# Two-layer gated cross-attention network on one core: in layer 0, two steps of TensorE put the per-token work last, and the sums of experts 4 to 7 are taken in other steps

## The chip, the cores and the metric

One Trainium2 chip (trn2), one core, one launch. The metric is the device time in microseconds; of the kernel before, three runs were taken, and their median is 2502.51 us (2501.88 to 2504.15). TensorE is called PE here, VectorE DVE, ScalarE ACT, GpSimd POOL and SyncE SP, as in the profile.

## What is computed

The input is 16 sequences (batches) of 256 tokens with 256 features, and a context of the same shape. Two layers follow each other; each is a cross-attention to the context and then a feed-forward part, both added to the stream through a tanh gate. The change lies wholly in layer 0:

```
x = x + tanh(g) * attention0(layernorm(x), ctx)      # 16 heads of 64, causal and padding mask
# layer 0, feed-forward, per token:
h = rmsnorm(layernorm(x));  q = h @ Wq + bq;  kv = (h @ Wdown + bdown) @ Wup + bup
att = softmax_over_g(q[head h] . k[head g] / 4)       # 16 x 16 scores of one token's own heads
x' = n + (sum_g att * v[head g]) @ Wo + bo            # n is layernorm(x)
h2 = rmsnorm(x');  gate = softmax(h2 @ Wg + bg)       # 8 experts
x = x + tanh(g) * (x' + sum_e gate_e * (h2 @ We[e]))
```

Layer 1 has an attention with 16 heads of 16 and a feed-forward part of three hidden products of 1024; the change doesn't touch it. Of layer 0's products, those marked hi and lo in the trace are three products each (a number is split in two parts, `product3`, lines 155 to 163).

## The kernel before, in words

**A software pipeline over batches.** In each round of layer 0 every engine works on three batches at once, a stage for each: the cross-attention of batch a, the per-token attention ("mix") of batch b = a-1, and the experts ("moe") of batch c = a-2; some projections of batch a+1 are made ahead. A round is the `body` of each engine (POOL from line 387, ACT, DVE, and PE from line 1021). It goes through 20 steps, s = 0 to 19 (STEPS = H + LAG_V = 20), roughly one attention head a step, with a beginning (BEGIN, BEGIN_OUT) and an end. Rounds 0, 1 and 2 are written out, rounds 3 to 14 are a hardware loop, and rounds 15 to 17 are written out again. The written-out ones from 15 on are merged with layer 1's programs by the numbers that the programs yield (`side_by_side`); SP's program yields 17 before the store of batch 13.

**Order on an engine.** Every engine executes its instructions in the order in which `body` writes them, so a wait holds up all that stands behind it. The engines meet by semaphores. What has to be followed:

- PE in a step: the scores of two heads in even steps (`pair_scores`, lines 945 to 948), then `beside_head` (the work of batches b and c), then the transposes of one head's probabilities (`head_transpose`, lines 955 to 957; in step 3 those of head 0 stand before `beside_head`), in odd steps from 5 on the value products of two heads (`pair_values`, lines 968 to 971), and then a projection: k3, v1, v3, q2, q3 of batch a in steps 0, 1, 2, 3, 5, and k0, xT, k1, v0, k2, v2 of batch a+1 in steps 9, 10, 11, 13, 16, 19. After step 19 comes the output projection (`attn_out`, line 980), and then the next round begins with the transposes of `o` (line 879, "oT"), q0, q1 and the product with `fo` ("out").
- `beside_head` on PE: step 2 transposes h; step 3 makes the per-token queries ("q", x is hT and w is fq); step 4 the down projection ("down") and the transposes of y ("h2T"); step 5 half of the up projection ("up0") and the gate's logits ("gate", wg); step 6 the other half ("up1"). An expert's product (`we0` to `we7`, 12 matmuls) is made in the steps of `expert_at`.
- DVE in a step: the masked scores and their maximum (`attn_max`, line 745), the reciprocal of the sum of the head before (`attn_sum`, line 751), and `beside_head`: adding bq to the queries (639), the low half of dT (645), adding bup to kv (651), an expert's gated sum into `acc` in the steps of `add_at` (`moe_experts`, line 729), the reduction of POOL's products to the per-token scores (`mix_scores`, line 655, in steps 7, 9, 11 and 12), its softmax (maximum 662 and subtraction 664 in step 12; sum 668, reciprocal 670 and multiplication 672 in step 13), and `mix_gather` (line 678) in steps 15, 16, 18 and 19.
- ACT in a step: transposed probabilities out of PSUM (485), exponential (468, 470), normalisation of the head before (476, 477), and, at the end of the step, the copies of projections (460), the exponential and scale of the gate (515 and 520 in steps 5 and 6), and the exponential of the per-token softmax (524, step 12).
- POOL: four multiplications of queries and keys (line 371), each of half a tile of tokens' heads, and four of weights and values (line 385, `weigh`), the first of which waits for the softmax (line 672); between the rounds the mask (354 to 358), powers (337) and the split of the context (344, 346).
- SP: the store of a batch (line 293) waits for `x2_ready`, which DVE gives after the sum of expert 7; behind it in SP's queue stand the loads of x, context and mask of a later batch (275, 278, 282).

**PSUM banks.** Products go to banks in rotation, and a user of a bank waits until the one before has been copied out. `attn` has two banks: the order of its uses is q0, q1, k3, v1, v3, T0, q2, T1, T2, q3, T3, ... (T0 is the transposes of head 0), after six uses that are made ahead. So k3, v3, q2 and T2 are in one bank, and v1, T0, T1 and q3 in the other. `side` has two banks too, in the order oT, out, hT, q, down, h2T, up0, gate, up1, we0 to we7, idle. `score` has three, `heads` one.

Of the kernel before, what the change touches and what calls it, by code (L numbers as in the profile page):

```python
# [121 lines left out]
def first(batch):  # L122

    return isinstance(batch, int) and batch == 0


def wait_apart(engine, passed, sem, value):

    engine.wait_ge(sem, value)
    engine.sem_inc(passed, 1)  # L130
# [36 lines left out]
def layer0(nc, ins, x2, left, right, both):  # L167
# [51 lines left out]
    attn = Banks(nc, left, both, "l0_attn", attn_uses + ["out"], ahead=["xT", "k0", "k1", "k2", "v0", "v2"])  # L219

    mix_at = {2: "hT", 3: "q", 4: "down", 5: "up0", 6: "up1"}
    expert_at = {6: 0, 7: 1, 8: 2, 10: 3, 12: 4, 14: 5, 15: 6, 17: 7}
    add_at = {7: 0, 8: 1, 9: 2, 10: 3, 12: 4, 14: 5, 15: 6, 17: 7}
    score_at = {7: 0, 9: 1, 11: 2, 12: 3}

    gather_at = {15: 0, 16: 1, 18: 2, 19: 3}
# [44 lines left out]
    def sync(sp):  # L271
        def load(b):
            if not first(b):
                sp.wait_ge(xn_ready, b)
            sp.dma_start(xin[:], ins["x"][bass.ds(b, 1)][0]).then_inc(x_in, 16)
            if not first(b):
                sp.wait_ge(ctx_ready, b)
            sp.dma_start(ctxin[:], ins["ctx"][bass.ds(b, 1)][0]).then_inc(ctx_in, 16)

            if not first(b):  # L280
                wait_apart(sp, sp_passed, mask_ready, b)
            sp.dma_start(maskbits[:], ins["mask"][bass.ds(b, 1)].to_broadcast([P, S])).then_inc(mask_in, 16)

        def load_residual(b):

            if not first(b):
                sp.wait_ge(x1_copied, b)
                sp.wait_ge(h_ready, b)
            sp.dma_start(x1[:], ins["x"][bass.ds(b, 1)][0]).then_inc(xres_in, 16)

        def store(b):
            sp.wait_ge(x2_ready, b + 1)
            sp.dma_start(x2[bass.ds(b, 1)][0], acc[:]).then_inc(x2_stored, 16)

        load(0)
        for k, (src, _hi, _lo, rows) in enumerate(splits):
            if k >= 2:
                sp.wait_ge(split_lo, k - 1)
            sp.dma_start(stage[0:rows, k % 2, 0:src.shape[1]], src).then_inc(raw_in[k % 2], 16)
            if k == 1:  # L300
                for dst, src in params:
                    sp.dma_start(dst, src).then_inc(params_in, 16)
            if k == 2:
                load_residual(0)
                sp.dma_start(wo[:].rearrange("p c n -> p (c n)"), ins["wo"]).then_inc(wo_in, 16)
            if k == 3:
                load(1)
        load(2)
        load_residual(1)
        with sp.Fori(3, B) as b:  # L310
            load(b)
            load_residual(b - 1)
            store(b - 3)
        load_residual(B - 1)
        yield 17
        store(B - 3)
        yield 40.6
        store(B - 2)
        yield 52
        store(B - 1)  # L320
# [549 lines left out]
    def tensor(pe):  # L870
        T = nc.tensor

        def transpose4(banks, use, batch, src):

            ps, full, free, turn = banks.at(use, batch)
            pe.wait_ge(free, turn)
            for c in range(ND):
                for t in range(NT):
                    last = T.transpose(ps[:, c * S + t * P:c * S + (t + 1) * P], src[:, t, c * P:(c + 1) * P], ident[:])
            last.then_inc(full, 1)  # L880

        def features(use, a, w, x):

            j = int(use[1:])
            ps, full, free, turn = attn.at(use, a)
            pe.wait_ge(free, turn)
            for u in range(2):
                m = slice((2 * j + u) * P, (2 * j + u + 1) * P)
                last = product3(nc, ps[:, u * S:(u + 1) * S],
                                [(w[0][:, c, m], w[1][:, c, m], x[0][:, c, :], x[1][:, c, :]) for c in range(ND)])  # L890
            last.then_inc(full, 1)

        def values(j, a):
            t, m = j // 2, slice((j % 2) * 512, (j % 2 + 1) * 512)
            ps, full, free, turn = attn.at(f"v{j}", a)
            pe.wait_ge(free, turn)
            product3(nc, ps[:], [(cT[0][:, c, t * P:(t + 1) * P], cT[1][:, c, t * P:(t + 1) * P], wv[0][:, c, m], wv[1][:, c, m])
                                 for c in range(ND)]).then_inc(full, 1)
# [24 lines left out]
        def moe_experts(c, j):  # L923
            moe_product(f"we{j}", c, [w[:, :, j * D:(j + 1) * D] for w in we], D)
# [58 lines left out]
        def project(use, a):  # L983

            if use == "xT":
                pe.wait_ge(xn_ready, a + 1)
                transpose4(attn, "xT", a, xn)
            elif use[0] == "q":
                features(use, a, wq, xT)
            elif use[0] == "k":  # L990
                if use == "k0":
                    pe.wait_ge(ctx_ready, a + 1)
                features(use, a, wk, cT)
            else:
                values(int(use[1:]), a)

        def beside_head(b, c, s):

            if b is not None and s in mix_at:
                use = mix_at[s]  # L1000
                if use == "hT":
                    pe.wait_ge(h_ready, b + 1)
                    transpose4(side, "hT", b, h)
                elif use == "q":
                    side.emptied(pe, "hT", b)
                    tokens(side, "q", b, hT, fq, D)
                elif use == "down":
                    mix_down(b)
                else:
                    mix_up(b, int(use[2:]))  # L1010
            if c is not None:
                if s == 4:
                    pe.wait_ge(h2_ready, c + 1)
                    transpose4(side, "h2T", c, y)
                elif s == 5:
                    side.emptied(pe, "h2T", c)
                    moe_product("gate", c, wg, E)
                elif s in expert_at:
                    moe_experts(c, expert_at[s])

        def body(a, b, c, nxt):
            yield BEGIN
            if c is not None:
                pe.wait_ge(gathered, 4 * (c + 1))
                transpose4(side, "oT", c, o)
            if a is not None:
                attn.emptied(pe, "xT", a)
                project("q0", a)
                project("q1", a)
            yield BEGIN_OUT  # L1030
            if c is not None:
                side.emptied(pe, "oT", c)
                tokens(side, "out", c, foT, fo, D)
            if a is not None:
                attn.emptied(pe, "v2", a)
                attn.emptied(pe, "q0", a)
            for s in range(STEPS):
                yield s
                if a is not None and s < H and s % 2 == 0:
                    if s % 4 == 0 and s > 0:  # L1040
                        attn.emptied(pe, f"q{s // 4}", a)
                    if s == 12:
                        attn.emptied(pe, "k3", a)
                    pair_scores(a, s)
                if a is not None and s == LAG_T:
                    head_transpose(a, 0)
                beside_head(b, c, s)
                if a is not None:
                    if LAG_T < s < H + LAG_T:
                        head_transpose(a, s - LAG_T)  # L1050
                    if s >= LAG_V0 and s % 2 == 1:
                        if s - LAG_V0 == 8:
                            for use in ("v1", "v3"):
                                _, _, emptied, turn = attn.at(use, a)
                                wait_apart(pe, pe_passed, emptied, turn + 1)
                        pair_values(a, s - LAG_V0)
                    if s in own_at:
                        project(own_at[s], a)
                if nxt is not None and s in ahead_at:
                    project(ahead_at[s], nxt)  # L1060
            yield STEPS
            if b is not None:
                side.skip(pe, "idle", b)
            if a is not None:
                score.skip(pe, "idle0", a)
                score.skip(pe, "idle1", a)
            if a is not None:
                heads.emptied(pe, "o2", a)
                heads.emptied(pe, "o3", a)
                attn_out(a)  # L1070
# [835 lines left out]
```

## Time and profile before

| | |
|---|---|
| median of three runs | 2502.51 us |
| the profiled execution's own time | 2502.84 us |
| its span in the trace | 2501.0 us |
| mean granted clock of PE | 0.961 |
| busy: PE, DVE, ACT, POOL | 89%, 59%, 51%, 41% of the span |

The first half of the span is layer 0, about 78 us a round; rounds of layer 1 follow from some 1300 us on. The profile gives a start and a duration to each instruction, the idle time of its engine before it in brackets, and behind "<-" the instruction that ended this idle time. A matmul of the same length lasts about twice as long when the granted clock is 0.5. Ends of matmuls are modelled and overlap with the next start, so for PE the distance from start to start is the better measure.

### The profile page before, as it was taken

The numbers are of one execution on the slowest core, as the hardware profiler recorded it, in microseconds if no ns is written. First come the engines' busy times: TensorE is split into PE (matmuls) and PEld (weight loads), VectorE is DVE, ScalarE is ACT, GpSimd is POOL, SyncE is SP. The second block draws the span as 40 slices with busy tenths as digits, with TensorE's granted clock in tenths as the row PEclk, the third lists the DMA queues.
The fourth block names the chain that finished last, engine by engine and source line by source line (L and its number), as shares of the span: only waits on it lengthen the run. The fifth ranks groups of instructions, "written<-read, shape, count | busy, mean of one in ns | idle before, by whom it ended". The sixth has DMA issues, their size and how long they took to land.

```text
span 2501.0 us, 47888 instructions
## 1 busy us (share of the span) xinstructions
PE 2227.4 (89%) x16000; PEld 1887.5 (75%) x16000; DVE 1480.4 (59%) x3922; ACT 1267.7 (51%) x3969; POOL 1023.1 (41%) x907
## 2 busy tenths in 40 slices
PE   5888899898888888888875799999999999999998
PEld 4667677777777777777664688888888888888888
DVE  4466666767667676676767635555555555555551
ACT  5655655556555565555633434455544444445541
POOL 1255555565555655556446213333332322333320
PEclk9999999999999999999977799999999999999999
DMA  4000000000000000000110200000000000000000
GB/s 154 8 12 14 6 17 17 17 13 4 17 17 17 13 4 17 17 17 4 39 32 13 110 16 7 13 17 17 17 17 17 17 17 16 5 13 17 17 9 9
DMA packets 26000, 51.40 MB, mean 21 GB/s; under 512 B 6160, under 2 KB 7312, under 8 KB 24784
## 3 DMA queue, kind: packets, MB, share of 16 engines
q1 hardware_dynamic: 25936, 50.57, 6.0%
q8 instruction: 37, 0.61, 0.1%
q14 instruction: 27, 0.22, 0.0%
HBM read 42.17 MB, written 8.39 MB: 20 GB/s over the span
## 4 chain that ended last, share of the span: by engine, by line
PE 57%; DVE 15%; ACT 8%; POOL 6%; issue 6%; DVEq 4%; POOLq 2%; DMA 0%; ACTq 0%
PE l_ffn L1714 13%; POOL l_prod L385 5%; PE l_ffn L161 4%; PE l_attn L161 4%; PE l_ffn L162 4%; PE l_ffn L163 4%; PE l_attn L1675 4%; PE l_attn L163 3%; PE l_attn L162 3%; DVEq L735 3%; PE l_side L161 3%; PE l_heads L1689 2%; POOLq L355 2%; PE l_side L163 2%; PE l_side L162 2%
## 5 line engine op out<-in xcount | busy, mean ns | idle before, releaser
L1253 POOL TENSOR_SCALAR l_probs<-l_probs,l_rinv 128x256 f32<-128x256 f32 x512 | 240.3, 484 | 479.2 <-DVE l_rinv L1492 478.3
L1376 ACT ACTIVATE l_probs<-l_score,l_negmax 128x256 f32<-128x256 f32 x512 | 239.1, 474 | 268.2 <-DVE l_negmax L1487 268.1
L385 POOL TENSOR_TENSOR l_prod<-l_att,l_kv 128x2048 f32<-128x2048 f32 x64 | 288.5, 4542 | 164.6 <-DVE l_att L672 164.6
L371 POOL TENSOR_TENSOR l_prod<-l_q,l_kv 128x2048 f32<-128x2048 f32 x64 | 291.2, 4561 | 150.7 <-DVE l_att L655 86.6
L1714 PE MATMUL l_ffn<-l_w,l_hid 128*128 128x256 f32 x1536 | 348.6, 381 | 1.0 <-ACT l_hid L1337 1.0
L1714 PEld LDWEIGHTS l_ffn<-l_w,l_hid 128*128 128x128 f32 x1536 | 286.2, 190 | 48.8 <-issue 12.7
L1499 DVE COPY l_probsT<-l_attn 128x512 f32<-128x512 f32 x240 | 164.5, 686 | 142.8 <-PE l_attn L1675 142.8
L745 DVE CUSTOM_DVE_ANT_0 l_probs<-l_score,l_mbias 128x256 f32<-128x256 f32 (+1 forms) x512 | 161.3, 352 | 144.9 <-PE l_score L947 95.8
L678 DVE TENSOR_REDUCE l_h<-l_prod 128x128 f32<-128x2048 f32 x64 | 146.3, 2286 | 107.5 <-POOL l_prod L385 107.2
L468 ACT ACTIVATE l_probs<-l_probs,l_negmax 128x256 f32<-128x256 f32 x256 | 130.8, 511 | 107.7 <-DVE l_negmax L745 106.6
L1487 DVE TENSOR_REDUCE l_negmax<-l_score 128x2 f32<-128x512 f32 x256 | 175.0, 684 | 15.0 <-PE l_score L1663 13.7
L485 ACT COPY l_probsT<-l_attn 128x384 f32<-128x384 f32 x256 | 120.9, 472 | 112.8 <-PE l_attn L957 112.7
L1337 ACT ACTIVATE l_hid<-l_ffn,l_b 128x256 f32<-128x256 f32 x384 | 162.1, 482 | 19.4 <-PE l_ffn L163 18.1
L1675 PE MATMUL l_attn<-l_ident,l_probs 128*128 128x128 f32 x1024 | 157.1, 279 | 11.4 <-DVE l_probsT L1499 6.6
L161 PE MATMUL l_side<-l_we_hi,l_h2T_hi 128*128 128x256 f32 x512 | 159.8, 312 | 2.2 <-DVE l_acc L729 1.8
L161 PE MATMUL l_attn<-l_cT_hi,l_wk_hi 128*128 128x256 f32 x384 | 124.0, 323 | 40.6 <-DVE l_xT_lo L609 39.0
L655 DVE TENSOR_REDUCE l_att<-l_prod 128x128 f32<-128x2048 f32 x64 | 145.8, 2279 | 5.0 <-issue 4.4
L162 PE MATMUL l_side<-l_we_lo,l_h2T_hi 128*128 128x256 f32 x512 | 147.5, 288 | 0.0
L163 PE MATMUL l_side<-l_we_hi,l_h2T_lo 128*128 128x256 f32 x512 | 147.1, 287 | 0.0
L476 ACT ACTIVATE l_probs<-l_probs,l_rinv 128x256 f32<-128x256 f32 x256 | 127.6, 498 | 24.3 <-DVE l_rinv L751 24.3
L1675 PEld LDWEIGHTS l_attn<-l_ident,l_probs 128*128 128x128 f32 x1024 | 118.8, 143 | 25.4 <-issue 12.4
L1238 POOL TENSOR_TENSOR l_rstdF<-l_varF,l_neghalf 128x2 f32<-128x2 f32 x16 | 11.2, 701 | 303.1 <-DVE l_varF L1421 303.1
(261 smaller groups left out, 7177.2 us busy)
## 6 DMA issues: line engine op xcount, KB each, us to landing
l_ctxin<-in_ctx SPq DMA_DIRECT2D x32, 256.0 KB, 3.0
l_xin<-in_x SPq DMA_DIRECT2D x16, 256.0 KB, 2.6
l_x<-in_x SPq DMA_DIRECT2D x16, 256.0 KB, 2.6
x<-l_acc SPq DMA_DIRECT2D x16, 256.0 KB, 2.0
l_xin<-x SPq DMA_DIRECT2D x16, 256.0 KB, 3.1
l_x<-x SPq DMA_DIRECT2D x16, 256.0 KB, 2.6
out<-l_x SPq DMA_DIRECT2D x16, 256.0 KB, 2.0
l_hid<-in_w SPq DMA_DIRECT2D x2, 1536.0 KB, 8.2
```

What stands on the lines that cost most here:

```text
L161: last = nc.tensor.matmul(out, wh, xh, start=n == 0, stop=False)
L162: last = nc.tensor.matmul(out, wh, xl, start=False, stop=False)
L163: last = nc.tensor.matmul(out, wl, xh, start=False, stop=n == len(terms) - 1)
L371: nc.gpsimd.tensor_tensor(prod[:, u].rearrange("p (h g d) -> p h g d", h=half, g=H), q4[:, u * half:(u + 1) * half].unsqueeze(2).to_broadc ...
L385: nc.gpsimd.tensor_tensor(prod[:, u].rearrange("p (h d g) -> p h d g", h=half, d=HD), a4.unsqueeze(2).to_broadcast([P, half, HD, H]), v4.u ...
L1253: last = nc.gpsimd.tensor_scalar(probs[:, j % 4, t * S:(t + 1) * S], probs[:, j % 4, t * S:(t + 1) * S], rinv[:, j, t:t + 1], 1.0, ALU.mul ...
L1337: last = nc.scalar.activation(hid[:, c, :], ps[:, u * S:(u + 1) * S], ACT.Relu, bias=b1[:, c:c + 1])
L1376: last = nc.scalar.activation(probs[:, s % 4, t * S:(t + 1) * S], ps[:, t * S:(t + 1) * S], ACT.Exp, bias=negmax[:, s, t:t + 1], accum_out ...
L1487: V.tensor_reduce(negmax[:, j], ps[:].rearrange("p (t k) -> p t k", t=NT), axis=AX.X, op=ALU.max, negate=True).then_inc(max_ready, 1)
L1499: V.tensor_copy(probsT[:, j % RING, :], ps[:]).then_inc(free, 1)
L1675: last = T.transpose(ps[:, kt * S + t * P:kt * S + (t + 1) * P], probs[:, j % 4, t * S + kt * P:t * S + (kt + 1) * P], ident[:])
L1714: last = T.matmul(ps[:, 0:D], hid[:, c, t * P:(t + 1) * P], w2[:, c, :], start=c == 0, stop=c == 3 * NHC - 1)
```

## The change

The per-token queries in step 3, and up0 and the gate's logits in step 5, are issued by PE last in their step: behind q2's projection, and behind T2, the value products of heads 0 and 1 and q3's projection. Expert 4 is made in step 13 for step 12, and expert 6 in step 16 for step 15; experts 5 and 7 keep their steps. DVE adds experts 4 to 7 in steps 14, 15, 17 and 18 for 12, 14, 15 and 17, so that steps 12 and 13 have no sum of an expert. SP's program yields 18.5 for 17 ahead of the store of batch 13.

```diff
-    expert_at = {6: 0, 7: 1, 8: 2, 10: 3, 12: 4, 14: 5, 15: 6, 17: 7}
-    add_at = {7: 0, 8: 1, 9: 2, 10: 3, 12: 4, 14: 5, 15: 6, 17: 7}
+    expert_at = {6: 0, 7: 1, 8: 2, 10: 3, 13: 4, 14: 5, 16: 6, 17: 7}
+    add_at = {7: 0, 8: 1, 9: 2, 10: 3, 14: 4, 15: 5, 17: 6, 18: 7}
...
         load_residual(B - 1)
-        yield 17
+        yield 18.5
         store(B - 3)
...
                     head_transpose(a, 0)
-                beside_head(b, c, s)
+                if s not in (3, 5):
+                    beside_head(b, c, s)
                 if a is not None:
                     if LAG_T < s < H + LAG_T:
                         head_transpose(a, s - LAG_T)
...
                     if s in own_at:
                         project(own_at[s], a)
+                if s in (3, 5):
+                    beside_head(b, c, s)
                 if nxt is not None and s in ahead_at:
                     project(ahead_at[s], nxt)
```

## Rows read from the trace of the kernel before

**Rows 1.** The page, part 5: busy, mean ns of one, idle before, releaser.
```profile
L371 POOL TENSOR_TENSOR l_prod<-l_q,l_kv 128x2048 f32<-128x2048 f32 x64 | 291.2, 4561 | 150.7 <-DVE l_att L655 86.6
```

**Rows 2.** Timeline of DVE: the softmax's subtraction, the fourth and the thirteenth of sixteen.
```profile
376.50 0.69 DVE L664 TENSOR_TENSOR l_att<-l_att,l_amax 128x512 f32<-128x512 f32 x1
...
1081.73 0.69 DVE L664 TENSOR_TENSOR l_att<-l_att,l_amax 128x512 f32<-128x512 f32 x1
```

**Rows 3.** Chain that ended last, 940 to 1020 us: start, us, what.
```profile
946.42 2.30 DVE l_h L678
...
962.18 0.49 DVE l_hT_lo L613
...
982.07 2.35 DVEq L735
...
999.18 0.48 DVE l_acc L729
...
1006.73 11.48 POOL l_prod L385 x3
```

**Rows 4.** Timeline of PE: T0, q, q2, up0, gate, and the scores of step 6.
```profile
961.15 0.33 PE L955 MATMUL l_attn<-l_ident,l_probs 128*128 128x128 f32 x1 [0.46 <-ACT l_v L460]
...
962.71 0.39 PE L161 MATMUL l_side<-l_fq_hi,l_hT_hi 128*128 128x256 f32 x1 [1.02 <-DVE l_hT_lo L613]
...
964.24 0.28 PE L161 MATMUL l_attn<-l_xT_hi,l_wq_hi 128*128 128x256 f32 x1
...
968.70 0.47 PE L161 MATMUL l_side<-l_fup_hi,l_dT_hi 64*128 64x512 f32 x1 [0.40 <-DVE l_dT_lo L645]
...
969.91 0.24 PE L161 MATMUL l_side<-l_wg_hi,l_h2T_hi 128*128 128x8 f32 x1 [0.28 <-DVE l_h2T_lo L613]
...
974.12 0.48 PE L945 MATMUL l_score<-l_kT,l_qT 64*128 64x256 f32 x1
```

**Rows 5.** Timeline of ACT: the copies of v1, of v3, and of T1.
```profile
960.45 0.56 ACT L460 COPY l_v<-l_attn 128x512 f32<-128x512 f32 x1
...
963.21 0.57 ACT L460 COPY l_v<-l_attn 128x512 f32<-128x512 f32 x1
...
968.74 0.48 ACT L485 COPY l_probsT<-l_attn 128x384 f32<-128x384 f32 x1
```

**Rows 6.** Timeline of DVE, from the maximum to the scores' reduction in step 12, two rounds.
```profile
528.06 0.08 DVE L745 DVE_READ_ACCUMULATOR2_ANT l_negmax<- 128x1 f32 x1
...
530.02 2.29 DVE L655 TENSOR_REDUCE l_att<-l_prod 128x128 f32<-128x2048 f32 x1 [0.16 <-issue]
...
997.98 0.08 DVE L745 DVE_READ_ACCUMULATOR2_ANT l_negmax<- 128x1 f32 x1
...
1000.22 2.29 DVE L655 TENSOR_REDUCE l_att<-l_prod 128x128 f32<-128x2048 f32 x1 [0.16 <-issue]
```

**Rows 7.** Timeline of PE: its other long stalls in a round.
```profile
915.08 0.39 PE L161 MATMUL l_attn<-l_cT_hi,l_wk_hi 128*128 128x256 f32 x1 [2.47 <-DVE l_xT_lo L609]
...
936.74 0.33 PE L955 MATMUL l_attn<-l_ident,l_probs 128*128 128x128 f32 x1 [1.23 <-ACT l_kT L460]
...
937.95 0.40 PE L968 MATMUL l_heads<-l_probsT,l_v 128*64 128x256 f32 x1 [0.66 <-ACT l_probsT L485]
...
948.85 0.65 PE L879 MATMUL l_side<-l_ident,l_h 128*128 128x128 f32 x4 [1.53 <-DVE l_h L678]
```

**Rows 8.** Stretches: busy time of PE, PEld, DVE, ACT, POOL, then granted clock, DMA.
```profile
962.70:966.10 3.40, 3.39 (x28) 3.23 (x30) 3.10 (x12) 3.38 (x11) 0.48 (x1) 1.00 0.02 7
...
523.30:526.70 3.40, 3.40 (x16) 3.09 (x18) 2.72 (x6) 2.21 (x8) 1.05 (x1) 0.50 0.00 0
...
547.20:550.60 3.40, 3.40 (x9) 2.69 (x9) 1.99 (x4) 1.00 (x2) 3.40 (x2) 0.50 0.21 77
```

**Rows 9.** Timeline of SP's store, and of POOL's first use of the context.
```profile
470.63 0.36 SPq L293 DMA_DIRECT2D x<-l_acc  x1
...
490.99 0.60 POOL L344 CAST l_cT_hi<-l_ctxin 128x512 fp32r<-128x512 f32 x1
```

## The prediction

> **What bounds the kernel now.** I read the page first: PE is the busiest engine, yet a busy PE proves nothing here, since each engine waits for each in turn. The change touches layer 0 only, so the second view is DVE's timeline at one fixed point of the round: nine rounds from 376.50 to 1081.73 us are 78.36 us each [rows 2]. Third, the chain that ended last, through one round [rows 3]. It should be read as the list of works of which a microsecond saved is a microsecond of the round. It runs through the last reduction of the products (946.42), ACT's and DVE's work on head 0 and hT (962.18), then PE from the queries of step 3 to the scores of step 6, through expert 4's sum in step 12 (999.18), the softmax, and POOL's weighing (1006.73 on). So both places of the change lie on the chain, and I price them there by the timelines of PE, ACT and DVE. PE has slack at the end of a round: it idles 1.53 us before it may transpose `o` [rows 7].
>
> **Part one: sums of experts out of steps 12 and 13.** In step 12 DVE has its maximum at 528.14 and starts the last reduction of scores at 530.02, or, in a later round, at 998.06 and 1000.22 [rows 6]: 1.88 and 2.16 us, in which it waits for expert 4 from PE and adds it. Without the sum, one short reciprocal stands between (under 0.2 us). The gain is 1.7 to 2.0 us, and I take 1.9. All that follows to POOL's first weighing waits for this reduction alone, or for the softmax's own exponential on ACT, which also gets its work sooner, since expert 4 no longer stands before T9 on PE. So POOL starts 1.9 us sooner, its products follow each other without a gap (the 11.48 us of the chain [rows 3]), and the last reduction, with which the next round starts, comes 1.9 us sooner.
>
> The moved sums cost nothing: steps 14 and 15 have one each as before, and those of steps 17 and 18 (about 0.9 us each, two halves of 0.48 as in the chain's row [rows 3]) lie in DVE's waits for POOL, about 4.5 us a product (the weighing is as long as the other multiplication [rows 1]) less 2.30 us for its reduction [rows 3]; were that cover gone, they would cost 0.9 each. On PE expert 4 goes past T9 only, and v0's projection stands behind it, but at step 14 PE has done the same work as before; expert 6 goes past T12 and the value products of heads 10 and 11, which start sooner. Each finds its bank free, two sums back. Expert 7's bank is next used by oT, and oT waits for the reduction of step 19, behind the sum of step 18 anyway. Its sum comes one step later, and so do SP's store and the loads of x and context behind it in the queue; the context was used 20.4 us after the store [rows 9], so a delay of some 1 us is covered.
>
> Must PE follow with the output projection? It has 1.53 us of slack, and the stalls before it, 1.23 and 0.66 us, wait for ACT behind the sum of head 15, which stands on DVE behind the first reduction of weighed products [rows 7]. That comes 1.9 us sooner, so the stall of 1.23 goes and PE follows. The part holds in the 14 rounds that have all of batch c and batch b: 14 x 1.9 = 26.6 us gained.
>
> **Part two: steps 3 and 5 on PE.** Before, T0 has started at 961.15 and PE waits 1.02 us for hT, then makes q from 962.71 and q2 from 964.24 (1.53 us each) [rows 4]. It looks as if q2 could fill this wait. But q2 writes the bank that v3 had, and ACT copies v3 out only from 963.21 to 963.78 [rows 5]. ACT's copies are not moved by the change. With the 0.14 us from v1's copy (961.01) to T0's start [rows 4, 5], q2 starts at 963.92, q at 965.45, and the scores of step 4 at 966.98; before, they could start at 965.77. The reordered step **loses 1.2 us**: 1.02 us of wait becomes 2.2.
>
> Step 5 gives a part back. Before, up0 waits 0.40 us for dT and the gate's logits 0.28 for h2T [rows 4]; now T2, the value products and q3 stand before them and cover both. But the value products need T1's copy, which ACT ended at 969.22 [rows 5] and, behind h2T's high half, ends 1.2 later, at 970.4. PE is then through T2 at about 970.0 and waits some 0.4 us, again for ACT. The rest is 0.8 for the value products, 1.6 for q3, 0.8 for up0 and 1.3 for the logits (start to start in step 5 of this trace), so the scores of step 6 start at about 975.0, against 974.12 [rows 4]: **0.9 us lost a round**. Bounds: 1.2 (nothing given back) and 0.5 (the wait for T1's copy covered).
>
> What is late next: up0 comes at 972.9 for 968.70, so kv is ready at about 974.5, and POOL's two first products of 4.56 us [rows 1] end at 983.6. The third waits for DVE's first reduction, which ended at 984.42 [rows 3] and will end 0.9 later; 1.7 us are left. DVE, which takes q's sum before the statistics of the next batch, is late in steps 4 and 5 by about 2 us and idles before the scores of step 6 anyway. The gate's exponential on ACT fits before T3. This part holds in the 15 rounds that have batches a and b: 15 x 0.9 = 13.5 us lost, and before any effect of the clock the sum is -13.1 us.
>
> **The clock.** After PE's stall of 2.47 us [rows 7], and so in 523.30 to 526.70, the granted clock was 0.50, which is 1.2 GHz, its lower level; after the two idle times of 0.46 and 1.02 us it stayed at 1.00, which is 2.4 GHz; after 1.2 and 0.66 us, T15 between them, it was 0.50 in one round [rows 7, 8]. The new idle times at step 3 are 0.46 and 2.2 us with T0 between them: nearer to the stall that is followed by the lower level in each steady round. A stretch of 3.40 us at 0.50 does the work of 1.70; on the chain from step 3 to step 6 I take 1.5 of it, with 0 and 1.7 as ends. The trace doesn't show how often it would fall. I take ten of fifteen rounds, and five rounds in which the stall before k1 now keeps the clock, as it stayed up after the two stalls of 1.2 and 0.66 us in some rounds and not in others [rows 7, 8]: 5 x 1.5 = +7.5 us net.
>
> The Trainium skill ("TensorE: Matmul & The Clock Gate", in "Why this matters for your kernels") speaks of idle gaps longer than any of these as what puts the clock back. By this rule the gap of 2.2 us costs no clock, and the time would be that of the first rival below; the trace disagrees for 2.47 us, which was followed by 0.50 [rows 7, 8].
>
> **Sum**: 2502.84 - 26.6 + 13.5 + 7.5 = 2497.2 for the profiled execution. It stood 0.3 above the median, so the forecast is 2497 us. With other clocks the same case gives 2491 to 2505.
>
> **The rivals.**
> - **The clock holds at step 3.** For it: the gap is shorter than 2.47. Against: with 0.46 before it, it is longer in sum. The sum is then -13.1, or -20.6 where five rounds also spare k1's low stretch: 2482 to 2490 us.
> - **The clock falls in each round at step 3 and is spared nowhere** (slower). For it: after k1's stall it fell in each steady round. 15 x 1.5 - 13.1 = +9.4: 2512 us. The other side begins at 13.1 / 1.5, some nine net stretches, and counts as slower from twelve.
> - **The softmax's gain is swallowed at the end of the round**: PE's output projection becomes the bound after its slack of 1.53 us, if the stalls of rows 7 don't go. -14 x 1.53 + 13.5 + 7.5 = -0.4: 2502 us.
> - **The change does at step 3 what it seems to do**, q2 filling the wait, because ACT's copy of v3 would be done: a gain of up to 1.02 + 0.68 us in place of the loss, 15 x 1.7 + 26.6: 2450 us. Against: rows 5.
>
> **How the numbers follow.** A measurement of this kernel can tell about 0.2%, 5 us. Forecast case 0.45 (faster 0.22, same 0.23), first rival 0.23, second 0.20 (slower 0.15, same 0.05), third 0.10 (half same, half slower, as the clock falls), fourth 0.02. Faster 0.47, same 0.33, slower 0.20. The range takes in the first two rivals but for a thin edge: 2483 to 2511 us; the forecast case's own is 2491 to 2505.
>
> **What would show it.** PE: a stall of about 2.2 us before q2's first matmul, ended by ACT's copy of v (line 460), no stall before q; a stall of about 0.4 before the value products of step 5, none before up0 or the gate. DVE: line 655 in step 12 right behind the maximum, no line 729 in steps 12 and 13; the time from line 664 to POOL's line 385 unchanged; no stall of 1.23 before T15. The clock: 0.50 behind step 3 in some rounds. It is wrong if q2 starts without a wait, if the stall before `o`'s transposes goes to zero, or if the period changes by other than -1.0 us plus 1.5 us for each added low stretch.

## The result, and the profile after

The changed kernel takes **2515.09 us** (median of six runs, 2511.85 to 2521.07) against 2502.20 us (six runs of the kernel before, 2498.61 to 2505.89): a ratio of 1.0054, with a 95% interval of 1.0037 to 1.0070. It is 13 us slower, outside the forecast range of 2483 to 2511 us. The profiled execution took 2511.85 us, with a span of 2510.1 us and a mean granted clock of 0.953 (0.961 before).

First the rounds. DVE's timeline of the changed kernel, at the same two rounds as [rows 2]:

```profile
383.10 0.69 DVE L664 TENSOR_TENSOR l_att<-l_att,l_amax 128x512 f32<-128x512 f32 x1
...
1097.26 0.69 DVE L664 TENSOR_TENSOR l_att<-l_att,l_amax 128x512 f32<-128x512 f32 x1
```

Nine rounds now take 79.35 us each, for 78.36. Where does the microsecond go? PE's timeline of one round, from T0 (the transposes of head 0) to the scores of step 6, to be laid beside [rows 4]:

```profile
976.82 0.32 PE L955 MATMUL l_attn<-l_ident,l_probs 128*128 128x128 f32 x1 [0.47 <-ACT l_v L460]
979.51 0.38 PE L161 MATMUL l_attn<-l_xT_hi,l_wq_hi 128*128 128x256 f32 x1 [2.15 <-ACT l_v L460]
...
986.11 0.40 PE L968 MATMUL l_heads<-l_probsT,l_v 128*64 128x256 f32 x1 [0.74 <-ACT l_probsT L485]
...
988.51 0.50 PE L161 MATMUL l_side<-l_fup_hi,l_dT_hi 64*128 64x512 f32 x1
...
989.41 0.27 PE L161 MATMUL l_side<-l_wg_hi,l_h2T_hi 128*128 128x8 f32 x1
...
990.84 0.48 PE L945 MATMUL l_score<-l_kT,l_qT 64*128 64x256 f32 x1
```

q2 stalls for 2.15 us, ended by ACT's copy of v; the value products of step 5 stall for 0.74, ended by ACT's copy of T1; up0 and the logits no longer wait. From T0 to the scores of step 6 it is 14.02 us for 12.97: 1.05 us lost where the clock stays up. Nearly all of it is lost in step 3: the scores of step 4 start at 982.50, 5.68 us behind T0, where they started at 965.76, 4.61 us behind it. Step 5 loses and wins nothing. ACT's timeline has the two copies that end these stalls:

```profile
978.88 0.58 ACT L460 COPY l_v<-l_attn 128x512 f32<-128x512 f32 x1
...
985.49 0.48 ACT L485 COPY l_probsT<-l_attn 128x384 f32<-128x384 f32 x1
```

Then the softmax, where DVE's last reduction of scores now follows the maximum at once, for 1.9 to 2.2 us later in [rows 6]:

```profile
1015.26 0.42 DVE L745 CUSTOM_DVE_ANT_0 l_probs<-l_score,l_mbias 128x256 f32<-128x256 f32 x1
...
1015.89 2.27 DVE L655 TENSOR_REDUCE l_att<-l_prod 128x128 f32<-128x2048 f32 x1
```

And PE's later stalls, beside [rows 7]:

```profile
1012.54 0.39 PE L161 MATMUL l_attn<-l_cT_hi,l_wk_hi 128*128 128x256 f32 x1 [1.88 <-DVE l_xT_lo L609]
...
1030.82 0.32 PE L955 MATMUL l_attn<-l_ident,l_probs 128*128 128x128 f32 x1 [0.67 <-ACT l_kT L460]
...
1035.76 7.14 PE L980 MATMUL l_attn<-l_wo,l_qT 128*128 128x256 f32 x32 [1.27 <-PEq L95]
1042.92 0.54 PE L879 MATMUL l_side<-l_ident,l_h 128*128 128x128 f32 x3
```

The stall of T15 has halved. New is the one of 1.27 us ahead of the output projection. Its releaser is line 95, PE's idle use of a side bank (it waits for the bank to be free and passes it on), and that bank was last used by expert 6, whose sum DVE now takes from 1033.74 to 1034.61. PE's idle time before it transposes `o`, 1.53 us before, is gone, which the prediction had named as a sign of being wrong.

The clock, in the view by stretches (busy time of PE, PEld, DVE, ACT and POOL, then granted clock, DMA share, GB/s), for fourteen rounds and for the stretch behind the logits of the round above; the first fence is the kernel before:

```profile
140.20:1237.80 1097.60, 966.67 (x6790) 799.46 (x6787) 758.99 (x2142) 634.33 (x1985) 595.06 (x237) 0.97 0.05 15
```

```profile
144.70:1252.10 1107.40, 974.83 (x6781) 815.22 (x6778) 762.92 (x2141) 632.93 (x1985) 595.72 (x237) 0.95 0.05 15
...
991.10:997.90 6.80, 6.80 (x33) 6.01 (x32) 2.32 (x13) 2.24 (x9) 6.80 (x2) 0.52 0.00 0
```

PE is at 1.2 GHz for longer: the trace's clock records give 113 us in those rounds for 75 before. In nearly all of the 6.80 us behind the logits the level was the lower one, though nothing had stalled for more than 0.74 us since q2.

What such a stretch costs depends on where it lies. Of the next two rounds, both of the kernel before, the first has a low stretch behind T15 and one behind the stall of k1, the second only the one behind k1:

```profile
454.87:533.15 78.28, 70.15 (x490) 58.14 (x488) 54.63 (x154) 45.43 (x142) 42.53 (x17) 0.96 0.04 14
611.47:689.85 78.38, 68.71 (x490) 56.99 (x488) 54.55 (x155) 45.47 (x142) 42.54 (x17) 0.98 0.04 14
```

They are equally long, so the stretch behind T15 cost nothing; in the first, PE's idle time of 1.53 us before it transposes `o` is missing instead. By place, over fourteen rounds, with a double stretch counted as two (the softmax part alone is the first experiment below):

| low stretches | before | softmax part alone | changed |
|---|---|---|---|
| behind the stall of step 3 | 0 | 0 | 13 |
| behind the logits of step 5 | 7 | 10 | 14 |
| behind the stall of k1 | 10 | 11 | 4 |
| elsewhere | 5 | 1 | 2 |

Last, a thing that I had not looked for. In most rounds line 601 (DVE's normalisation for the next batch, two instructions) takes 0.74 us. In four of the changed kernel's it takes 2.0 us. Timelines of DVE and POOL, first of the kernel before, then of the changed one:

```profile
971.06 9.10 POOL L371 TENSOR_TENSOR l_prod<-l_q,l_kv 128x2048 f32<-128x2048 f32 x2 [3.93 <-DVE l_kv L651]
...
981.16 0.74 DVE L601 TENSOR_SCALAR l_xn<-l_xin,l_mvA,l_rstdA 128x256 f32<-128x256 f32 x2
```

```profile
753.27 9.11 POOL L371 TENSOR_TENSOR l_prod<-l_q,l_kv 128x2048 f32<-128x2048 f32 x2 [5.08 <-DVE l_kv L651]
...
760.86 1.99 DVE L601 TENSOR_SCALAR l_xn<-l_xin,l_mvA,l_rstdA 128x256 f32<-128x256 f32 x2
```

Before, POOL's pair of products ended at 980.16, one microsecond ahead of line 601. Now kv is ready later and the pair ends at 762.38, and DVE's pair ends at 762.85: POOL's end plus one instruction of line 601 (0.41 us). The slow ones are those that start well within a product of POOL; where they don't, in the other ten of the fourteen rounds, they take 0.74 us.

### The profile page after: what moved, and what is told of

Its sections match the earlier page's. It is cut to its first block, busy times and chain, and to the rows that moved or that the text cites. A ratio compares the mean times of both kernels' runs of the same rounds, so it can differ in the third digit from the quotient of the medians.

```text
span 2510.1 us, 47888 instructions
## 1 busy us (share of the span) xinstructions
PE 2236.6 (89%) x16000; PEld 1903.4 (76%) x16000; DVE 1489.8 (59%) x3922; ACT 1264.9 (50%) x3969; POOL 1022.2 (41%) x907
## 4 chain that ended last, share of the span: by engine, by line
PE 59%; DVE 16%; ACT 9%; POOL 6%; issue 6%; DVEq 3%; DMA 0%; PEldq 0%; ACTq 0%; POOLq 0%
PE l_ffn L1717 13%; POOL l_prod L385 6%; PE l_ffn L161 4%; PE l_attn L980 4%; PE l_ffn L162 4%; PE l_ffn L163 4%; PE l_attn L1678 4%; PE l_attn L161 3%; DVE l_att L655 3%; PE l_attn L163 3%; PE l_attn L162 3%; PE l_heads L1692 3%; PE l_side L161 3%; PE l_side L163 2%; PE l_side L162 2%
## 5 line engine op out<-in xcount | busy, mean ns | idle before, releaser
L161 PE MATMUL l_side<-l_we_hi,l_h2T_hi 128*128 128x256 f32 x512 | 166.7, 326 | 2.0 <-DVE l_acc L729 1.9
L162 PE MATMUL l_side<-l_we_lo,l_h2T_hi 128*128 128x256 f32 x512 | 153.4, 300 | 0.0
L161 PE MATMUL l_attn<-l_xT_hi,l_wq_hi 128*128 128x256 f32 x384 | 120.0, 313 | 37.1 <-ACT l_v L460 33.8
L163 PE MATMUL l_side<-l_we_hi,l_h2T_lo 128*128 128x256 f32 x512 | 153.1, 299 | 0.0
```

The source lines that it names most:

```text
L161: last = nc.tensor.matmul(out, wh, xh, start=n == 0, stop=False)
L162: last = nc.tensor.matmul(out, wh, xl, start=False, stop=False)
L163: last = nc.tensor.matmul(out, wl, xh, start=False, stop=n == len(terms) - 1)
```

## The experiments

The two theories I set out with: **A**, the reordered steps 3 and 5 lose (through ACT's copy of v3, with the clock behind it) and the softmax part gains; **B**, the softmax part's gain is lost again at the end of the round, by the new wait for expert 6's sum. Each kernel was compared with the kernel before in the same sitting (medians 2500.7 to 2501.7 us).

**The softmax part alone.** The changed kernel, with PE's order in steps 3 and 5 as before:

```diff
-                if s not in (3, 5):
-                    beside_head(b, c, s)
+                beside_head(b, c, s)
...
-                if s in (3, 5):
-                    beside_head(b, c, s)
```

> The change without its first half: PE's order in steps 3 and 5 is that of before. Theory A (steps 3 and 5 lose, the softmax part gains): 1.7 to 2.0 us gained in each of 14 rounds, so 20 to 28 us below the kernel before, T0 to the scores of step 6 at 12.97 us as before. Theory B (the softmax's gain is lost again at the end of the round, because PE's output projection now waits for the sum of expert 6 through the idle use of its bank): no more than 0 to 8 us below before, and a stall ahead of line 980 that sets the next round's start.

Measured: 2481.06 us, ratio 0.9911 (0.9891 to 0.9932), 21 us faster. Its DVE in step 12:

```profile
985.06 0.28 DVE L745 CUSTOM_DVE_ANT_0 l_probs<-l_score,l_mbias 128x128 f32<-128x128 f32 x1
985.35 2.27 DVE L655 TENSOR_REDUCE l_att<-l_prod 128x128 f32<-128x2048 f32 x1
```

Fourteen rounds take 1076.0 us for 1097.6, with the same 75 us at the lower clock. But these lie elsewhere (the table above): in ten rounds the clock now falls behind the logits, with PE's order there as it was. Such a stretch is not free, as a round with one low stretch (behind k1) and a round with a second behind the logits show:

```profile
525.72:602.24 76.52, 69.01 (x492) 57.19 (x492) 54.52 (x154) 45.42 (x142) 42.73 (x17) 0.98 0.04 14
988.47:1066.44 77.97, 69.92 (x489) 57.70 (x489) 54.51 (x154) 45.48 (x142) 42.65 (x17) 0.96 0.04 14
```

A holds, and so B can't be the cause of the loss: the stall ahead of line 980 is in this kernel too (1.30 us).

**The order of steps 3 and 5 alone.** The PE hunks of the change on the kernel before.

> The first half alone: experts and their sums as before. Theory A: at least 15 x 1.05 = 16 us slower than before, and with low clock stretches behind step 3 or at step 6 (about 1.5 us each) and the normalisation of xn beside POOL's product (1.25 us) 25 to 45 us slower. Theory B: about 13 us slower, the whole of what was measured.

Measured: 2554.96 us, ratio 1.0196 (1.0178 to 1.0214): 53 us slower, well beyond my 45. The two halves are not additive: -21 and +53 make +32, where together they measured +13. Here the lower clock takes 150 us of fourteen rounds, 75 us more than in the kernel before; the changed kernel has 38 us more than the softmax part alone. At half speed that can cost up to 38 and 19 us, and with 15 us at full clock (14 x 1.05) it makes up the 53 and the 34. Why more stretches fall in the one than in the other is not shown.

**Only step 5, with the softmax part.** `if s != 5:` and `if s == 5:` in place of the tuples.

> The change with step 3 as before, so only step 5 is reordered. If the low clock at step 6 comes from what PE does there (up0, the logits of 8 columns, the scores and up1 in a row, with no dense product between), it is there in most rounds though nothing stalls 2.15 us in step 3, and the time is 0 to 15 us above the softmax part alone. If it comes from step 3's stall, there is none, and the time is within 5 us of the softmax part alone.

Measured: 2484.09 us, ratio 0.9923 (0.9907 to 0.9940). Of PE's timeline and the stretches:

```profile
960.56 0.40 PE L968 MATMUL l_heads<-l_probsT,l_v 128*64 128x256 f32 x1 [0.73 <-ACT l_probsT L485]
...
963.86 0.27 PE L161 MATMUL l_side<-l_wg_hi,l_h2T_hi 128*128 128x8 f32 x1
```

```profile
965.70:972.50 6.80, 6.80 (x35) 6.03 (x32) 2.39 (x13) 2.67 (x11) 6.80 (x2) 0.53 0.00 0
```

Step 3 has only its old stall of 1.02 us, and yet the clock falls behind the logits, in twelve of fourteen rounds. That is not new with this order: the softmax part alone has it in ten. In the two rounds in which it stays up throughout, line 601 collides with POOL and the stall before k1 is 2.78 us for 2.47. From T0 to the scores of step 6 nothing is lost or won (49.15 us after line 664, as before). The 3 us above the softmax part alone are within the noise of the two.

**Only step 3, with the softmax part.** The same with 3.

> The change with step 5 as before, so only step 3 is reordered. q2 stalls 2.15 us, and 1.2 us are lost in each of 15 rounds (18 us) against the softmax part alone, and with low stretches behind the stall up to 22 us more. If the low clock at step 6 comes from the group in step 5, there is none at step 6 here.

Measured: 2519.77 us, ratio 1.0063 (1.0043 to 1.0084): 39 us above the softmax part alone, the upper end of what was expected. PE's timeline and the stretches:

```profile
979.18 0.39 PE L161 MATMUL l_attn<-l_xT_hi,l_wq_hi 128*128 128x256 f32 x1 [2.15 <-ACT l_v L460]
987.02 0.47 PE L161 MATMUL l_side<-l_fup_hi,l_dT_hi 64*128 64x512 f32 x1 [0.74 <-DVE l_dT_lo L645]
```

```profile
980.10:983.40 3.30, 3.30 (x18) 3.30 (x17) 0.00 (x0) 1.68 (x6) 0.00 (x0) 0.50 0.00 0
990.30:993.60 3.30, 3.30 (x18) 2.76 (x14) 0.00 (x0) 2.16 (x11) 3.30 (x2) 0.50 0.00 0
```

The low stretch behind the stall is there, and one behind the logits as well, which this order leaves where they were. **Step 3 alone costs as much as both steps together** (39 us for 34, within the spread of the two), and the last sentence of the expectation fell: both places have low stretches. No instance of line 601 in these rounds is slow in this kernel, so the loss doesn't need the collision with POOL.

**Line 601 in step 4.** In the changed kernel, DVE's line 601 moves to step 4, where POOL is idle and DVE ahead:

```diff
-                elif s == 7:
+                elif s == 4:
                     pre_normalise(nxt)
```

> The changed kernel, with DVE's normalisation of the next batch (line 601) in step 4 for step 7, where POOL is idle. Collision theory (line 601 takes 2.0 us in the rounds in which POOL's first two products still run, for 0.74 in the others): no instance over 0.8 us in the loop, and since 0.74 us leave the chain of step 7 too, 10 to 16 us below the changed kernel. If the longer line 601 is a mark of lateness and no cause, the round stays within 0.3 us and the time within 4 us.

Measured: 2499.73 us, ratio to the kernel before 0.9995 (0.9986 to 1.0004); against the changed kernel's 2515.09 that is 15 us less. All 32 instances of line 601 now take 0.40 to 0.41 us:

```profile
735.61 0.72 DVE L601 TENSOR_SCALAR l_xn<-l_xin,l_mvA,l_rstdA 128x256 f32<-128x256 f32 x2
```

So the longer line 601 was a collision and no mark of lateness. Its price isn't shown by this run: four rounds of 1.25 us would be 5 us and 0.74 us out of every round 10, but the lower clock also takes 102 us here for 113.

**The same move on the softmax part alone.**

> The softmax part alone, with the same move of line 601. It has no collision to remove, so only the 0.74 us of step 7 go: up to 10 us below the softmax part alone if the chain runs through them, nothing if the low stretches of the clock take them back.

Measured: 2462.66 us, ratio 0.9849 (0.9835 to 0.9862). That is 18 us below the softmax part alone, for up to 10 expected; the stall before k1 fell from 2.47 to 1.90 us, and fourteen rounds have 65 us at the lower clock for 75. This kernel had no collision to lose, and the move gained as much. With the move in both, steps 3 and 5 in the new order still cost 37 us (2499.73 and 2462.66 us), where they cost 34 with collisions: nothing shows that the collisions have a part in the loss.

**PE's idle bank use behind the projection.** In the changed kernel:

```diff
-            if b is not None:
-                side.skip(pe, "idle", b)
             if a is not None:
                 score.skip(pe, "idle0", a)
...
                 attn_out(a)
+            if b is not None:
+                side.skip(pe, "idle", b)
```

> The changed kernel, with PE's idle use of the side bank (which waits for the sum of expert 6) behind the output projection. The projection then starts right behind v2, the 1.3 us ahead of line 980 go, and PE idles them before it transposes o. Theory A (POOL's weighing ends the round): the time stays within 3 us. Theory B (the projection's late start ends it): 10 to 18 us faster.

Measured: 2510.92 us, ratio 1.0042 (1.0028 to 1.0055), an interval that overlaps the changed kernel's. PE's timeline:

```profile
1033.04 7.07 PE L980 MATMUL l_attn<-l_wo,l_qT 128*128 128x256 f32 x32
1041.68 0.65 PE L879 MATMUL l_side<-l_ident,l_h 128*128 128x128 f32 x4 [1.58 <-DVE l_h L678]
```

The stall went from ahead of line 980 to ahead of line 879, where POOL's weighing and DVE's reduction end it as before. The 10 to 18 us of theory B are not there; it falls.

**ACT copies v3 early.** The changed kernel, with one ACT instruction moved:

```diff
                 before_exp(b, c, s)
+                if a is not None and s == 2:
+                    project("v3", a)
...
-            if a is not None and s in own_at:
+            if a is not None and s in own_at and own_at[s] != "v3":
                 project(own_at[s], a)
```

> The changed kernel, with ACT's copy of v3 ahead of the exponential of head 2 in step 2. Theory A (q2 waits for this copy, and that is what step 3 loses): q2's stall falls from 2.15 to some 0.7 us, the scores of step 6 come 1.4 us sooner, and with fewer low stretches behind it the time falls by 20 to 40 us. Rival (the loss in steps 3 to 6 is the order of the up projection and logits alone): within 5 us.

Measured: 2479.97 us, ratio 0.9910 (0.9894 to 0.9925), 35 us below the changed kernel. PE's q2:

```profile
954.39 0.38 PE L161 MATMUL l_attn<-l_xT_hi,l_wq_hi 128*128 128x256 f32 x1 [0.58 <-ACT l_v L460]
```

The stall falls from 2.15 to 0.58 us, and there is no low stretch behind it in any of fourteen rounds. So it was the wait for this copy that made the reordering a loss. With the copy early, the new order takes as long as the old order with the copy late (2479.97 and 2481.06 us), though its rounds have 96 us at the lower clock for 75. The old order with the copy early was not run: q2 has no stall there that an early copy could shorten, but whether the new order is better than the old one with the copy early isn't shown.

**Both repairs together.**

> The changed kernel with both repairs: ACT's copy of v3 early, and line 601 in step 4. If the two are separate losses, their effects add: 35 and 15 us below the changed kernel, about 2465 us. If the low clock at step 6 takes the second one back, it stays at 2475 to 2480 us.

Measured: **2452.52 us**, ratio 0.9811 (0.9792 to 0.9830), the fastest that was run: 48 us below the kernel before and 63 below the changed one, for 50 expected. The repairs help each other: the two alone gave 35 and 15 us. Fourteen rounds have 61 us at the lower clock, for 96 with the early copy alone, where five of line 601's pairs are slow in these rounds; here none is.

**The same, step 5 in the old order.**

> The same with step 5 in the old order, so only step 3 is reordered. If the row of small products in step 5 is what lowers the clock at step 6, that stretch is gone here, and the time is at or below that of the softmax part with line 601 in step 4 (2463 us); if not, it is 5 to 15 us above the kernel with both steps reordered, since up0 and the logits wait for dT and h2T again.

Measured: 2458.49 us, ratio 0.9837 (0.9821 to 0.9852): 6 us above, though the two intervals overlap a little. The time fits both branches; the stretch decides for the second: it is there behind the logits in eleven of fourteen rounds, some 3 us sooner, as the logits are.

**q3's dense projection between the logits and the scores of step 6.** In the kernel with the softmax part and step 5 alone reordered:

```diff
-                    if s in own_at:
-                        project(own_at[s], a)
                 if s == 5:
                     beside_head(b, c, s)
+                if a is not None:
+                    if s in own_at:
+                        project(own_at[s], a)
```

> The softmax part with step 5 reordered, but q3's dense projection behind the logits and ahead of the scores of step 6. The work and the waits are the same. If the row up0, logits, scores, up1 without a dense product in it is what lowers the clock at step 6, then the low stretches there become fewer or single and the time falls by 3 to 12 us below 2484; if low clock comes from idle time alone, they stay and so does the time.

Measured: 2487.30 us, ratio 0.9947 (0.9933 to 0.9960), not below 2484. PE's first product of the logits, and a stretch that begins behind them:

```profile
963.93 0.27 PE L161 MATMUL l_side<-l_wg_hi,l_h2T_hi 128*128 128x8 f32 x1
```

```profile
964.80:975.00 10.20, 10.20 (x46) 9.05 (x46) 1.83 (x9) 2.07 (x10) 9.01 (x2) 0.50 0.00 0
```

In four rounds the clock falls 0.7 to 0.9 us after the first product of the logits and stays low for 10.2 us, through q3's dense products. My idea that a row of small products up to step 6 was needed is refuted. A low stretch at or behind the logits, wherever they are put, is in each of these kernels, but never in all rounds: here in seven of fourteen, in the kernel before in five.

**The same with line 601 in step 4.**

> The same with line 601 in step 4: 10 to 18 us below the kernel without that move, as for the softmax part alone (2481 to 2463 us), so some 2460 us.

Measured: 2455.62 us, ratio 0.9823 (0.9799 to 0.9847), 32 us less where 10 to 18 were expected. The lower clock takes 51 us of fourteen rounds for 96 without the move, and in six of them it never falls, though the same logits are made. One of these by stretches, and behind it a steady round of the kernel before:

```profile
894.60:968.90 74.30, 66.67 (x489) 55.52 (x489) 54.59 (x155) 45.44 (x142) 42.71 (x17) 1.00 0.05 15
```

```profile
924.97:1003.36 78.39, 68.71 (x490) 56.87 (x488) 54.57 (x155) 45.46 (x142) 42.58 (x17) 0.98 0.04 14
```

## Why the prediction was wrong

**The softmax part** had mechanism and sign right. DVE's wait of 1.9 us went, POOL started sooner, the round gained. I took 14 x 1.9 = 26.6 us and it measured 21. Rounds with one low stretch are 1.85 us shorter (76.5 for 78.4), but others now have a second one behind the logits and take 78.0; where the kernel before had a second one behind T15, it cost nothing.

**Steps 3 and 5 at full clock**: predicted 0.9 us a round, measured 1.05. The sum came near because two errors offset each other: step 3 loses 1.07 for 1.2, and step 5 gives nothing back for 0.3. q2's stall was forecast as 2.2 and is 2.15, ended by the copy named; the value products' as 0.4 and is 0.74. The rival in which q2 fills the wait is excluded.

**"What is late next: [...] 1.7 us are left"** left something out. I asked whether POOL's late products would hold up a product or a reduction. I did not ask which DVE instruction they would now overlap. Line 601 lay one microsecond behind them, and in four rounds it lost 1.25 us. The Trainium skill says in "SBUF — State Buffer", section "Who interferes with whom", that only the port pair shared by VectorE and GpSimd makes engines contend, and as an exclusive lock. The rows agree: the second instruction of line 601 ends 0.47 us after POOL's pair, and moving it away ends the effect. But nothing shows that it made the forecast wrong: the reordering costs as much without it (37 us for 34). One misreading stands beside it: the row that I took for DVE's first reduction, 982.07 in [rows 3], is a wait; DVE's timeline has the reduction from 981.81 to 984.09. It changes the slack by 0.3 us.

**"I take ten of fifteen rounds, and five rounds in which the stall before k1 now keeps the clock"** is the step that failed most. It put 5 x 1.5 = 7.5 us for the clock. Of the two counts themselves, ten rounds of fourteen do have a low stretch behind step 3, and k1's is there in four rounds for ten (and so, before, not in each round, as the prediction has it). But stretches can be double: behind step 3 they sum to 44 us, where I had ten of 3.40. And I had left out a second place: behind the logits the clock is low in ten rounds and for 48 us, where the kernel before had five rounds and 24 us, and the softmax part alone ten and 34. Net, 38 us more at the lower level, where I had 17. And I had counted as equal what isn't: five of the stretches before lay elsewhere, and the ones behind T15 cost nothing, so that their going spared nothing. My own rule, a period changed by -1.0 us plus 1.5 for each added low stretch, gives +0.3 us a round for the eight that nine rounds got more; measured is +0.99. Without the three behind T15 eleven were added, and the rule gives +0.8.

The sizes: the changed kernel is 34 us above the softmax part alone. About 15 of them are the full-clock loss (14 x 1.05), and the 19 that are left are as much as 38 us at half speed can cost. This splits up a measured difference and does not test it; that the same split fits the order alone (15 and 38 for 53) speaks for it. Against the forecast, the clock term is short by some 11 us, the softmax term by 6, and the full-clock term by 1. Of the prediction's cases the second rival, the clock falling in each round, came nearest at 2512 us. I gave it 0.20. Its number came near, its count didn't: the clock did not fall in each round at step 3, and it was spared at k1.

Open is what of PE's activity lowers the clock behind the logits: the experiments show the place, and that a dense product behind them doesn't prevent it, not the cause. Nor do they show why it falls in some rounds and not in others with the same work.

## What to carry to other kernels

Before a product is put first to fill a wait, ask who empties the bank that it writes, and when that engine gets to it: here one ACT copy, queued behind a head's exponential and another's normalisation, turned a 1.0 us wait into 2.15, and moving this copy alone was worth 35 us. When work on one engine gets later, list what it will newly run beside on the other engines, not only who waits for it; here one overlap stretched a pair of instructions from 0.74 to 1.99 us, if without a price in the whole that could be measured. And where TensorE's clock falls, price a reordering by the chain at full clock and by the time at the lower level separately, since the same edit cost 53 us in one surrounding and 34 in another, and ask of each low stretch whether it lies where PE had idle time to lose.

## What the runs showed of the hardware

- A DVE TENSOR_SCALAR from SBUF to SBUF (128x256, 0.41 us) behind a POOL TENSOR_TENSOR (4.56 us) waits for its end: 1.99 us for the pair instead of 0.74, and 0.72 where POOL is idle.
- After idle times of 0.47 and 2.15 us with the transposes of one head between, the granted clock fell to 1.2 GHz in ten of fourteen rounds; with 0.58 us for the 2.15, in none. The Trainium skill, "TensorE: Matmul & The Clock Gate", section "Why this matters for your kernels", names only longer gaps as what to avoid; the trace disagrees.
- In the kernels with step 5 reordered it also fell at or behind twelve products of 8 columns (the logits), with no idle time on PE just before them, in seven to thirteen of fourteen rounds, and stayed low for up to 10.2 us of fully busy PE. That these products are the reason isn't shown.
- A low stretch behind T15, where PE had 1.53 us of idle time ahead, left the round as long as it was (78.28 and 78.38 us); in the softmax part alone, a second one, behind the logits, made it 1.5 us longer (77.97 for 76.52).
- A wait that DVE's sum of expert 6 ended at 1034.61 us let PE start its projection only at 1035.76. For the 1.15 us between, the trace names only PE's own queue (line 95); that they went into the waits and increments that the program has there is an inference.
